# Two groups of heads in one bank with one normalisation, and three of sixteen states accumulated by ScalarE and GpSimd

## The reference

```python
q, k, v = [(xn @ w + b).reshape(B, L, 16, 8) ...]
scores = einsum('bqhd,bkhd->bhqk', q, k) * 8 ** -0.5     # causal mask
attn_out = einsum('bhqk,bkhd->bqhd', softmax(scores), v).reshape(B, L, 128) @ o_w + o_b
...
dt = softplus(x_dbc[..., :R] @ dt_w + dt_b)
h = exp(dt * A) * h + (x * dt) * B_t                     # per channel and state, along L
y = einsum('bn,bdn->bd', C_t, h)                         # sum over the 16 states
ssm_out = ((y + x_c * D) * silu(z)) @ ssm_out_w
x = x + alpha * attn_out + (1 - alpha) * ssm_out
```

## Time and profile before

| | |
|---|---|
| median of 3 runs | 1694.33 us (1693.92 to 1700.46) |
| the profiled execution | 1693.45 us, of which the span of instructions is 1691.7 |
| mean granted TensorE clock | 0.933 of full speed |
| first scan to last scan | 124.7 to 851.1 us, 128 states |
| a steady batch (batch 4) | 486.80 to 581.04 us |
| attention alone, no work on DVE | 861.3 to 898.3 us |
| instructions | 22138 |

### The profile page before, as it was taken

The page is one execution under the profiler, slowest core; times in us unless marked ns, Lnnn a source line. Parts: engine busy times, 40 slices in busy tenths (PEclk is TensorE's granted clock), DMA queues, the critical chain, the costliest instruction groups (busy, mean ns, idle before and its releaser), DMA issues. The chain is left out here.

```text
span 1691.7 us, 22138 instructions
## 1 busy us (share of the span) xinstructions
PE 1443.8 (85%) x7228; PEld 896.1 (53%) x7228; DVE 1292.0 (76%) x1945; ACT 1095.7 (65%) x1840; POOL 838.1 (50%) x867
## 2 busy tenths in 40 slices
PE   3678898888989898888867988899999999888787
PEld 3234544444444444444423735687786877635673
DVE  2149998989898999989924858688676777748857
ACT  2465667686767777686655756778878788621017
POOL 3136677768585867768743213022222222238843
PEclk9787899999999999999998999899999999958989
DMA  3112222222222222222002110011111111000001
GB/s 89 45 38 82 77 71 68 78 74 69 67 68 65 74 73 67 79 75 74 26 1 70 43 47 26 29 50 44 40 48 38 44 44 44 26 1 0 1 1 50
DMA packets 61656, 84.74 MB, mean 50 GB/s; under 512 B 6589, under 2 KB 32039, under 8 KB 61543
## 3 DMA queue, kind: packets, MB, share of 16 engines
q1 hardware_dynamic: 61442, 83.30, 16.3%
q10 hardware_dynamic: 100, 0.03, 0.0%
HBM read 74.38 MB, written 8.78 MB: 49 GB/s over the span
## 5 line engine op out<-in xcount | busy, mean ns | idle before, releaser
L1756 POOL TENSOR_TENSOR dBx<-dtx,Bb 128x512 f32<-128x512 f32 x256 | 319.4, 1270 | 10.9 <-DMA Bb<-b_dram 9.5
L1352 DVE TENSOR_TENSOR hl<-lsq,hh 128x512 fp32r<-128x512 f32 x320 | 262.6, 831 | 80.7 <-ACT hh L1641 72.4
L1322 DVE TENSOR_TENSOR_SCAN hy<-bank,dBx 128x512 f32<-128x512 f32 x256 | 297.9, 1203 | 19.1 <-ACT bank L1625 12.9
L1638 ACT ACTIVATE lsq<-bank,vcol 128x512 f32<-128x512 f32 x320 | 219.0, 692 | 105.5 <-DVE hl L1352 65.0
L1047 PE MATMUL bank<-QK 127*128 127x128 bf16 (+7 forms) x1024 | 234.4, 311 | 50.0 <-DVE Mx L1312 26.4
L1775 POOL TENSOR_TENSOR stage<-stage,lrs 128x512 f32<-128x512 f32 x64 | 90.5, 1414 | 312.2 <-DVE lrs L1432 312.2
L1312 DVE TENSOR_REDUCE Mx<-bank 128x1 f32<-128x384 f32 (+3 forms) x352 | 213.6, 627 | 41.1 <-PE bank L1047 40.0
L1047 PE MATMUL bank<-x,we1h 128*128 128x512 f32 x640 | 211.0, 412 | 18.0 <-ACT hh L1641 9.8
L1566 ACT ACTIVATE PT<-bank 128x512 f32<-128x512 f32 x320 | 184.5, 593 | 49.1 <-PE bank L1047 46.4
L1625 ACT ACTIVATE bank<-dtv,alog 128x512 f32<-128x512 f32 x256 | 170.5, 691 | 52.1 <-DVE hy L1322 51.3
L1258 DVE SCALAR_TENSOR_TENSOR hy<-bank,bc,hy 128x256 f32<-128x256 f32 x480 | 198.0, 473 | 3.9 <-PE bank L1174 3.1
(11 more groups left out here) (256 smaller groups left out, 2430.4 us busy)
## 6 DMA issues: line engine op xcount, KB each, us to landing
Bb<-b_dram SPq DMA_DIRECT2D x128, 256.0 KB, 3.6
stage<-w_rows SPq DMA_DIRECT2D x64, 256.0 KB, 3.3
parts<-part SPq DMA_DIRECT2D x16, 384.0 KB, 2.7
QK<-parts SPq DMA_DIRECT2D x64, 96.0 KB
QK<-parts SPq DMA_DIRECT2D x64, 64.0 KB
stage<-in_L_ffn_We_dram SPq DMA_DIRECT2D x16, 256.0 KB, 3.3
hy<-in_L_attn_x_dram SPq DMA_DIRECT2D x8, 256.0 KB, 5.4
QK<-parts SPq DMA_DIRECT2D x64, 32.0 KB
```

Source lines behind the costliest of these rows:

```text
L1322: engine.tensor_tensor_scan(hst[:, 2 * (g % 3) + h, :], bank[4 + h][:], dBx[:, g % 4, h, :], 0.0, ALU.mult, ALU.add).then_inc(sems["dve_sc ...
L1352: engine.tensor_tensor(hl[:, sl, :], full[:, f, :], hh[:, sl, :].bitcast(F32), ALU.subtract).then_inc(sems["dve_hl"], 1)
L1638: engine.activation(full[:, f, :], o[:], fn, bias=bias).then_inc(sems["act_up"], 1)
L1756: engine.tensor_tensor(dBx[:, sl, h], dtx[:, b % 2, h], Bb[:, sl], ALU.mult).then_inc(sems["pool_dbx"], 1)
```

## The change

**One bank for two groups.** The columns of Vb move up by 9, so that head h stands at 9 + 9 h. The first group of a unit is multiplied as before with windows of 32 columns, which now begin one head early: its values fall on rows 9 to 16 of each 32, its row sums on row 17. The second group is multiplied into the same bank 3 with 9 columns, and overwrites rows 0 to 8. It does not wait for the bank. `normalise` runs once per unit, after the second group; seld spreads row 8 over rows 0 to 8 and row 17 over rows 9 to 17. wo is laid out to match, and one matmul does what two did. Its load takes eight DMAs where four were, and seld three selects where one was.

**Three states beside.** In batches 2 to 7, for n = 4, 8 and 12, the four scaled additions on DVE are replaced: ACT scales the transposed state out of the two banks into yB (four instructions of 128x256; yB lies in nT, slots 0 and 1), and POOL adds yB to yT, one instruction of 128x512 for each half. The next accumulation on DVE waits for POOL, now half by half.

```diff
+BESIDE = (4, 8, 12)
...
     def weigh(b, g, units):
         k = 3
-        it = step("weigh", b=b, g=g, bank=k, free=free.get(f"b{k}"), ready=(r_v[b], [(x, y) for _, _, x, y in units]),
+        it = step("weigh", b=b, g=g, bank=k, free=None if g % 2 else free.get(f"b{k}"), ready=(r_v[b], [(x, y) for _, _, x, y in units]),
...
-        it["o"] = free["Os"] = free[f"lrs{gg}"] = r_on[g] = up("pool_on")
+        it["o"] = free["Os"] = free[f"lrs{hf}"] = on = up("pool_on")
         for _ in range(4):
             yield
-        if gg == 0:
-            return
         k = take()
-        it = step("wo", b=b, g=g, bank=k, free=free.get(f"b{k}"), on=(r_on[g - 1], r_on[g]), h=h_last[b] or r_n[b])
-        it["m"] = free["On0"] = free["On1"] = up("pe_wo")
+        it = step("wo", b=b, g=g, bank=k, free=free.get(f"b{k}"), on=on, h=h_last[b] or r_n[b])
+        it["m"] = free[f"On{hf}"] = up("pe_wo")
...
-                later.append(normalise(b, g, m))
+                if g % 2:
+                    later.append(normalise(b, g, m))
...
+    nT_read = ("pe_qk", 12), ("pe_val", 2), ("pe_bx", 8)
...
             it = step("acc", g=g, half=half, bank=k, free=free.get(f"b{k}"), ready=ssm[b]["h", n], bc=ssm[b]["bc"],
-                      y_free=free.get("yT"), y_last=ssm[b]["y"])
+                      y_free=free.get("yT"), y_last=ssm[b]["y"][half], beside=b >= 2 and n in BESIDE, yb_free=free.get(f"yB{half}", nT_read))
             it["m"] = up("pe_ht")
-            it["y"] = free[f"b{k}"] = up("act_y") if n == 0 else up("dve_y", 2)
-            if half:
-                ssm[b]["y"] = it["y"]
+            it["y"] = free[f"b{k}"] = up("act_y") if n == 0 or it["beside"] else up("dve_y", 2)
+            ssm[b]["y"][half] = it["y"]
+            if it["beside"]:
+                it["z"] = ssm[b]["y"][half] = free[f"yB{half}"] = up("pool_y")
...
+        yB = nT[:, 0:2, :].rearrange("p a (b c) -> p (a b) c", c=256)
...
-                        x = mm(o[32 * i:32 * i + 32, P * kj:T], Vb[:, b % 2, kj, 36 * g + 9 * i:36 * g + 9 * i + 32],
+                        c0, m = 36 * g + 9 * i + 9 * (g % 2), 9 if g % 2 else 32
+                        x = mm(o[32 * i:32 * i + m, P * kj:T], Vb[:, b % 2, kj, c0:c0 + m],
                                PT[:, sl, off:off + n], start=(kj == 0), stop=(kj == 3), pos=(0, 32 * i))
...
-                    q.wait_ge(("ld_wo", 64), it["on"], it["free"])
-                    mm(o[:], wo[:, it["g"] - 1, :], On[:, 0, :], start=True, stop=False)
-                    mm(o[:], wo[:, it["g"], :], On[:, 1, :], start=False, stop=True).then_inc(sems["pe_wo"], 1)
+                    q.wait_ge(("ld_wo", 128), it["on"], it["free"])
+                    mm(o[:], wo[:, it["g"] // 2, :], On[:, it["g"] // 2, :]).then_inc(sems["pe_wo"], 1)
...
-                elif kind == "acc" and it["g"] % 16:
+                elif kind == "acc" and it["g"] % 16 and not it["beside"]:
...
-                elif kind == "acc" and it["g"] % 16 == 0:
-                    b = it["g"] // 16
-                    q.wait_ge(it["m"], it["y_free"], it["bc"])
+                elif kind == "acc" and (it["g"] % 16 == 0 or it["beside"]):
+                    b, n = divmod(it["g"], 16)
+                    q.wait_ge(it["m"], it["yb_free"] if n else it["y_free"], it["bc"])
...
-                        x = engine.activation(yT[:, j, :], o[:, 256 * jj:256 * jj + 256], ACT.Copy, scale=bc[:, b % 2, j, 0:1])
+                        x = engine.activation((yB if n else yT)[:, j, :], o[:, 256 * jj:256 * jj + 256], ACT.Copy, scale=bc[:, b % 2, j, n:n + 1])
...
-            engine.affine_select(out=sel, in_=sel, compare_op=ALU.not_equal, fill=1.0, base=-8, pattern=[[-32, 4], [0, 32]],
-                                 channel_multiplier=1).then_inc(sems["pool_set"], 1)
+            for c0, c1, row in ((0, 9, 8), (9, 18, 17), (18, 32, 8)):
+                engine.affine_select(out=sel[:, :, c0:c1], in_=sel[:, :, c0:c1], compare_op=ALU.not_equal, fill=1.0, base=-row,
+                                     pattern=[[-32, 4], [0, c1 - c0]], channel_multiplier=1).then_inc(sems["pool_set"], 1)
...
+                elif kind == "acc" and it["beside"]:
+                    j = 2 * it["half"]
+                    t = yT[:, j:j + 2, :]
+                    q.wait_ge(it["y"], it["y_last"])
+                    engine.tensor_tensor(t, t, yB[:, j:j + 2, :], ALU.add).then_inc(sems["pool_y"], 1)
...
-                engine.dma_start(wo[32 * i:32 * i + 8, :, :], d["L0_attn_o_w"].rearrange("(g i d) n -> i d g n", i=4, d=8)[i]).then_inc(sems["ld_wo"], 16)
+                for f, row in ((0, 9), (1, 0)):
+                    engine.dma_start(wo[32 * i + row:32 * i + row + 8, 0:2, :],
+                                     d["L0_attn_o_w"].rearrange("(a f i d) n -> i f d a n", a=2, f=2, i=4)[i][f]).then_inc(sems["ld_wo"], 16)
```

More of the change, by code:

```diff
@@ L167, in plan_mixers @@
     ring = [0, 1, 2, 6, 7]
-    r_parts, r_v, r_qk, r_mr, r_on = {}, {}, {}, {}, {}
+    r_parts, r_v, r_qk, r_mr = {}, {}, {}, {}
     h_last = [None] * NB
@@ L236, in normalise @@
     def normalise(b, g, m):
-        gg, k = g % 2, 3
+        hf, k = g // 2, 3
         it = step("os", b=b, g=g, m=m, os_free=free.get("Os"))
@@ L243, in normalise @@
         k = take()
-        it = step("on", b=b, g=g, o1=o1, bank=k, free=free.get(f"b{k}"), lrs_free=free.get(f"lrs{gg}"), on_free=free.get(f"On{gg}"))
+        it = step("on", b=b, g=g, o1=o1, bank=k, free=free.get(f"b{k}"), lrs_free=free.get(f"lrs{hf}"), on_free=free.get(f"On{hf}"))
         it["m"] = up("pe_dn")
@@ L998, in on_set @@
             return {name: i + 1 for i, name in enumerate(names.split())}
-        pool_set = on_set("vrow qk0 qk1 qk2 qk3 wo id0 id om cm on ep mask0 mask idb idn sel0 sel bsum vb0 mr vb qz0 qz1 qz2")
+        pool_set = on_set("vrow qk0 qk1 qk2 qk3 wo id0 id om cm on ep mask0 mask idb idn sel0 sel1 sel2 sel bsum vb0 mr vb qz0 qz1 qz2")
         dve_set = on_set("row0 row1 sc0 sc1 neg abs sgn2 max sgn gate om1 av2 av3 A qbs")
@@ L1719, in gpsimd_program @@
             q.wait_ge(("pool_set", pool_set["mr"]))
-            engine.memset(Vb[:, :, :, 0:144].rearrange("p a t (h j) -> p (a t) h j", j=9)[:, :, :, 8:9], 1.0).then_inc(sems["pool_set"], 1)
+            engine.memset(Vb[:, :, :, 9:153].rearrange("p a t (h j) -> p (a t) h j", j=9)[:, :, :, 8:9], 1.0).then_inc(sems["pool_set"], 1)
             for j in range(3):
@@ L1738, in gpsimd_program @@
                 elif kind == "on":
-                    gg = it["g"] % 2
+                    hf = it["g"] // 2
                     q.wait_ge(it["e2"], it["on_free"])
-                    engine.tensor_tensor(On[:, gg, :], Os[:], rdn[:, gg, :], ALU.mult).then_inc(sems["pool_on"], 1)
+                    engine.tensor_tensor(On[:, hf, :], Os[:], rdn[:, hf, :], ALU.mult).then_inc(sems["pool_on"], 1)
                 elif kind in ("wo", "so"):
```

10 lines of the change are left out of this document (5 added, 5 removed).

## The result

| | before | after |
|---|---|---|
| median (range, runs) | 1694.49 us (1693.92 to 1700.46, 4) | 1671.85 us (1669.76 to 1673.37, 4) |
| the profiled execution | 1693.45 us, span 1691.7 | 1669.76 us, span 1668.0 |
| mean granted TensorE clock | 0.933 | 0.934 |
| first scan to last scan | 725.20 us | 710.63 us |
| start of the last scan to start of the last addition to hT | 47.09 us | 42.20 us |

The ratio is 0.9864 (95% interval 0.9837 to 0.9891): 22.6 us, 1.4% faster. The forecast was 1670 us.

The account below looks back on a forecast made before the run. The prediction took the bound to change by step: DVE, PE or ACT. Attention's 21.3 us plus the state part's 2.9 gave 24.2 us off 1693.45, 1669.2; the median's 0.9 us above made the forecast 1670 us, range 1654 to 1686.

Parts of the forecast that it names:

- wo of even units, step 6: Between scans of states 6 and 7: second wo matmul goes where PE has no gap; 6 x 1.0 = 6.0 us gained.
- seld of odd units, steps 7 to 8: First group's seld product goes, in PE's regime; 6 x 1.1 = 6.6 us gained.
- seld of even units, step 0: Seld product goes ahead of the yT transposes on PE, for which DVE waits 0.58 us; 7 x 0.5 = 3.5 us.
- the end: After 861 us, where PE, ACT and POOL wait for each other: two wo pairs halve, one seld product goes; 5.2 us.
- n = 4: Step 5, batches 2 to 6: DVE frees 1.57 us, but the next maxima's input comes from gapless PE; gain 0.
- n = 8: Step 9, ACT's regime, batches 2 to 6: scalings delay the small copy and PE's bcol matmul; cost 1.2 x 5 = 6.0 us.
- n = 12: Step 13, DVE's regime but POOL full, batches 2 to 6: gain 1.0 of 1.57 us each, 5.0 us.
- batch 7: Last batch, DVE at 87.38 of 91.34 us, no preparation beside it: three moved states gain 3 x 1.3 = 3.9 us.
- DVE as the bound all along: Rival: DVE's 28.3 us saving counts in full, giving 1645 us; chance 0.12.
- the chain over GpSimd on the path: Rival: accumulations behind moved ones wait for ACT and POOL, 9.0 us a batch, 45 us in all, 1718; chance 0.05.
- The clock rival: Less PE work in DVE's steps drops the clock, as in step 15; 6 x 0.8 = 5 us, 1675; chance 0.13.
- the planner hands out other banks: Rival: PE waits for banks that ACT frees late; priced only at n = 8, no chance of its own given.

Follow-up runs that it names:

- attention_alone: The changed kernel with no state moved to ScalarE and GpSimd, all of the attention part kept; 1676.32 us, ratio 0.9885 to the kernel before.
- seld_light: The kernel before, with one light constant bfloat16 matmul in place of the seld product of g = 2, ScalarE's work kept; 1693.73 us in one run.
- states_alone: The kernel before with only the moved states (n = 4, 8, 12 in batches 2 to 7); 1693.68 us, ratio 0.9997 to the kernel before.
- seld_twice_odd: The changed kernel with the product of seld and Os issued twice on PE in units of odd number; 1674.0 us in one run.

## Why the prediction was right, by its own steps

The time, the sign and the range were right. The sum was 24.2 us; the stretches that it priced gave 19.5, and the profiled total came so near by luck: the other stages ran 4.2 us faster in that execution. Most of its signs came as said: a steady batch of 92.54 us (91.5 to 92.5), 32.1 us without DVE (32), the bcol matmul waiting for ScalarE, accumulation 13 waiting for GpSimd.

| term | forecast, us | measured, us |
|---|---|---|
| wo of even units, step 6 | 6.0 | 5.0 |
| seld of odd units, steps 7 to 8 | 6.6 | 6.0, in steps 8 and 9 |
| seld of even units, step 0 | 3.5 | 2.1 |
| the end | 5.2 | 6.2 in `attention_alone`, and -1.3 in the changed kernel, at a lower clock |
| n = 4 | 0 | 0.1 |
| n = 8 | -6.0 | -5.6, and -1.6 for a clock drop |
| n = 12 | 5.0 | 3.9 |
| batch 7 | 3.9 | 4.7 |
| clock in step 15 | not in the sum | -1.1 |

The measured column adds up to 18.4; 1.65 more came from a clock drop in step 10 of batch 1 that the kernel before had and the changed one had not; -0.45 is batch 0; that makes 19.6, and 19.5 was measured. Left without the clock's terms, the attention part gave 19.3 of 21.3 us and the state part 3.1 of 2.9; the clock's terms took 2.4 us (4.0 lost, 1.65 gained).

- **wo: right place, wrong size.** Half of a pair of 1.99 us was taken, a duration, whose end overlaps with what follows. From its start to that of the next instruction the pair took 1.82 us (517.96 to 519.78) and the single matmul takes 0.96 (511.07 to 512.03 in `attention_alone`); 0.86 went, and step 6 shows 0.83 to 0.86. In the same way the product with seld, priced at 1.1 us, takes 0.92 from start to start (535.43 to 536.35).
- **seld in steps 7 and 8: right size, wrong engine.** "PE's regime" was read from step 8 with PE at 6.39 of 6.39. `seld_light` took the product off PE and got 0.06 us a batch. The two steps together belong to ScalarE, whose 1.17 us wait at the start of step 8 made its busy share look small (5.19 of 6.39). The sentence that Ln and Exp "keep ACT from holding that gain back" named the cause as a side condition. The Trainium skill, "Perfetto Trace Analysis", section "Identifying the Most-Contended Engine", says that matmul busy share is not a good measure of how close a kernel is to roofline, because pipelined instructions look smaller in the trace. What failed here is another reading of the same figure, which engine is late: PE was full in step 8 (6.39 of 6.39) and not the limit of steps 8 and 9.
- **seld in step 0: the mis-sized term.** The 0.58 us wait was read in batch 5, in a step with the clock at 0.93 (7.57 us long), and multiplied by seven. At a clock of 1.00 the same wait, in batch 4, is 0.15 us. Step 0 of batch 4 before, and of batches 4 and 5 after:

```profile
486.80:493.95 7.15, 6.02 (x46) 3.85 (x46) 7.00 (x13) 4.33 (x8) 5.63 (x8) 1.00 0.32 115
```

```profile
481.04:488.20 7.16, 6.49 (x47) 4.55 (x46) 6.99 (x13) 3.42 (x7) 5.42 (x9) 0.85 0.33 112
...
573.58:580.74 7.16, 6.43 (x49) 4.37 (x48) 6.99 (x12) 3.65 (x7) 5.36 (x9) 0.87 0.40 114
```

  With the product gone, step 0 lasts 7.16 us at a clock of 0.85 too. The edit is worth 0 at full clock and 0.2 to 0.8 us where the clock was down before, which it was in four of seven.
- **n = 4: right, and for the reason given.** PE's block begins 2.97 us behind scan 5 in both kernels (516.64 against a scan at 513.67, and 511.06 against 508.09), because it hangs on the maxima that stand ahead of accumulation 4:

```profile
511.06 0.39 PE L1050 MATMUL bank<-QK 128*128 128x256 bf16 x2 [1.11 <-DVE Mx L1315]
```

- **n = 8: right**, 1.1 us in place of 1.2, by the two waits named. Keeping it on DVE made the kernel 7.4 us faster.
- **n = 12: 0.79 in place of 1.0.** GpSimd was late as forecast; PE's wait of 0.24 us was not foreseen, and both hung on the addition.
- **Batch 7: full 1.57 each**, the upper bound, in its own steps.
- **The end: 6.2 in place of 5.2** for the edit alone. The changed kernel shows 4.9, with a lower clock behind the last scan (0.83 where `attention_alone` has 1.00). That this is the clock's price, and that the states brought it on, is not shown; in `states_alone` that stretch is 0.2 us longer than before.
- **The rivals.** DVE as the bound all along fell with `states_alone`; so did the chain over GpSimd on the path. The clock rival was partly true: step 15 stands at 5.06 to 5.48 us in five batches of the changed kernel, 1.1 us in all more than before, and one drop in step 10 costs 1.6; with the 1.3 us behind the last scan, if they are the clock's, 4.0 of its 5 us, part of it balanced by the drop of before that is gone (1.65). That the planner hands out other banks showed nowhere but at n = 8.

Open: why the clock drops come where they do. In the profiled executions they fell on the same steps in kernels with the same times ahead of them (step 10 of batch 1 in before and `states_alone`, of batch 3 in after and `seld_twice_odd`) and moved when the batches ahead became shorter; no run here varied PE's activity alone in that place. Nor does the kernel alone fix them: runs of the kernel before had mean clocks from 0.926 to 0.942.

## What to carry to other kernels

Cut the profile into steps between two instructions of the same kind and compare two kernels step by step: at full clock a step repeats to 0.02 us where the whole time scatters by up to 12 (1688.72 to 1700.46 us for the kernel before), and a change of 1 us in 1700 can be read. Follow what a step gives through the steps behind it: a wait can move on, as GpSimd's did from step 14 to step 15. A stretch in which an engine is busy all the time is not proof that it is the limit; look for the engine whose rows follow one another without a wait, above all one that began the stretch waiting. A saving counts from the point at which something late hangs on it: taking work off DVE gave nothing behind the maxima that PE's block waits for, and 0.65 to 0.91 us a batch ahead of them.
